# Output projection and norm moved into the attention heads' block, routed masks made by halves

## The chip, the cores and the metric

One core of a Trainium2 chip. The metric is the device time of one execution in microseconds; three runs of the kernel before gave a median of 1414.84 us (1413.32 to 1418.07).

## The reference

Two layers on 1024 tokens of width 256, each made of two attention-like parts and one feed-forward part, all with a residual and a layer norm without weights in front:

```python
x = x + attn_a0(layernorm(x))     # 16 heads of 16, biases and gates
x = x + ternary_ffn(layernorm(x)) # weights rounded to -1, 0, 1 times a scale
x = x + gated_delta(layernorm(x)) # linear attention, 6 heads
x = x + ternary_ffn(layernorm(x))
x = x + attn_a1(layernorm(x))     # 16 heads of 16, no mask
x = x + routed_ffn(layernorm(x))
x = x + latent_attn(layernorm(x)) # causal, rotary, 16 heads
x = x + routed_ffn(layernorm(x))
```

An attention part ends in `out = ctx @ Wproj.T + bproj`. The routed part is one shared gated feed-forward (704 hidden features) with a low-rank addition for each of 8 experts, of which each token takes two:

```python
topw, sel = jax.lax.top_k(x @ gate_w.T, 2)
topw = softmax(topw, axis=1)            # over the tokens
lo_up = 2 * (xt @ up_A[e].T @ up_B[e].T)
h_e = silu(base_up + lo_up) * (base_gate + lo_gate)
mixed_h += c[:, None] * h_e             # c: weight of expert e for this token
out = mixed_h @ w_down.T + lora_down
```

## The kernel before

Tokens lie in 8 tiles of 128 rows in `X` (`x_tokens`), their normed values, turned, in `XNT` (`xn_features`, two tiles of 128 features by 1024 tokens). Each part of the network is a block in which five engines run streams written by hand; semaphores order them, and no engine begins the next block before all have ended this one. PSUM has 8 banks of 512 columns.

**Heads** (`attention_heads`, from line 483; used by `attention16` and by `latent_attention`). 128 chunks (16 heads by 8 key tiles): PE makes scores, ACT takes their exp, PE multiplies by the values. Banks 4 to 6 are a ring that the row maxima's scores and the small `turn` steps share; bank 7 holds a head's sum. At the end ACT copies the last head's sum, `turn(HEADS + 1)` transposes it and DVE divides it (L695, L698) into `O` (`attended`).

**Projection** (`project_out`, L1113). A block of its own: PE transposes `O` in 4 groups of 4 (L1138), ACT copies each (L1155), PE multiplies each tile by `wo` (two products of 256 columns, L1145), DVE adds it to `X` (L1163). The next routed weights are loaded by SP in this block (in the second `attention16` only).

**Norm** (L77). By pairs of tiles: DVE takes statistics (L95) and aggregates (L100); ACT the root (L147); DVE the reciprocal (L105), the shift (L107) and the odd tile's rows (L109); ACT the even tile's rows (L150); PE transposes both (L161, 4 transposes) into bank p; ACT copies 512 columns to `XNT` (L142, `take`). In the projection PE does the first pair's transposes behind tile 5 (`pe_behind`), and ahead of the last pair one unread product of 512 columns (`keep_busy`, L173). ACT takes the roots in the order of the pairs, each behind the copy of the pair before last. Norms stand at the end of the loading of inputs, both ternary parts, the gated part's `project_out` (three products for each tile), both `attention16`, the first routed part and the latent part.

**Routed part** (`routed_ffn`, L2176). PE begins with the four first-rank products of token half 0 (`lora_part`, L2243, two records of 512 columns each) between the 8 tiles' logits (L2270), then the base products of pair 0 (L2258), the sum over rows (L2275), base products of pair 1. DVE meanwhile takes logits, top two, indices, the softmax's parts, and spreads each token's expert and weight over 128 columns, 16 instructions of 128 columns each (L2414, L2423). PE transposes these 32 tiles (L2286), ACT copies them (L2375), DVE subtracts the masks (L2435, 1024 columns) and masks the first-rank products (L2431). Then steps (p, k) for 11 pairs of feature tile and token half and for two slots: PE adds the second-rank products (L2309), ACT takes silu (L2383), DVE the gate product (L2443) and the hidden values (L2448), POOL the mix (L2363). The order of steps is (0,0), (1,0), (0,1), (2,0), (1,1) and so on; pairs share 3 sets of two banks.

## Time and profile before

| | us |
|---|---|
| median of 3 runs | 1414.84 |
| profiled execution | 1413.13 |
| its span | 1411.1 |
| PE busy | 1325.0 |
| DVE busy | 893.1 |
| ACT busy | 689.3 |

The span is the time from the first to the last instruction of the profiled execution. Busy shares are averages over stages; the granted clock of PE is 0.985 of 2.4 GHz over the whole span, with the 11th, 12th and 15th of 40 slices at 0.8.

### The profile page before, as it was taken

Reading aid. Unit: us, or ns where it says so; the run is one execution under the profiler, and the core shown is the slowest. Engines: PE = TensorE matmul, PEld = TensorE weight load, DVE = VectorE, ACT = ScalarE, POOL = GpSimd, SP = SyncE. Lnnn points to the kernel's source line nnn. Section 1 sums busy time; section 2 is a strip of 40 time slices with the busy share of each in tenths; the row PEclk is TensorE's granted clock in tenths of the full one; section 3 lists DMA queues with packets and bytes.
Section 4 is the critical chain, followed back from the end, with each engine's and each line's share of the span. In section 5 each row is a group of like instructions: output and inputs, shape, how many; then the busy total and the mean of one; then the engine's idle time right before and its main releaser. Section 6 shows DMA issues by size and latency. Waiting matters only on the chain. (4 is left out here: it accounts for less than half of the span.)

```text
span 1411.1 us, 33212 instructions
## 1 busy us (share of the span) xinstructions
PE 1325.0 (94%) x13887; PEld 741.7 (53%) x13895; DVE 893.1 (63%) x2159; ACT 689.3 (49%) x1038; POOL 278.5 (20%) x343
## 2 busy tenths in 40 slices
PE   8999998999679988999999989999899999989999
PEld 4455554475346774644555554446355555654436
DVE  5999993757486456759999736433656556526431
ACT  5678786636483226546777842111444444442110
POOL 5340522001420000052000000111533434200110
PEclk9999999999889989999999999999999999999999
DMA  4323300000300000032222030001200000000000
GB/s 98 67 42 69 66 3 21 15 2 1 120 1 4 16 1 16 1 64 36 36 36 36 2 118 0 1 0 26 46 13 19 14 14 15 8 1 0 0 0 30
DMA packets 33526, 37.50 MB, mean 27 GB/s; under 512 B 8722, under 2 KB 24194, under 8 KB 33378
## 3 DMA queue, kind: packets, MB, share of 16 engines
q1 hardware_dynamic: 33376, 35.38, 12.2%
q8 instruction: 110, 1.80, 0.5%
q14 instruction: 38, 0.31, 0.1%
q10 hardware_dynamic: 2, 0.00, 0.0%
HBM read 18.43 MB, written 1.07 MB: 14 GB/s over the span
## 5 line engine op out<-in xcount | busy, mean ns | idle before, releaser
L677 DVE TENSOR_REDUCE row_max_pieces<-psum 128x1 f32<-128x512 f32 (+3 forms) x672 | 406.9, 646 | 103.2 <-PE psum L565 101.2
L778 ACT ACTIVATE probs<-psum 128x1024 f32<-128x1024 f32 (+7 forms) x384 | 343.4, 900 | 199.9 <-PE psum L565 199.4
L624 PE MATMUL psum<-probs,v_ones 128*32 128x256 f32 (+1 forms) x2880 | 236.4, 362 | 8.8 <-POOL probs L554 4.4
L565 PE MATMUL psum<-q_all,k_head 97*32 97x512 f32 (+3 forms) x1536 | 176.9, 487 | 0.0
L565 PE MATMUL psum<-k_stack,q_stack 96*32 96x512 bf16 x2048 | 159.8, 379 | 3.3 <-issue 3.2
L565 PE MATMUL psum<-q_stack,k_stack 97*32 97x512 bf16 x2048 | 158.0, 379 | 2.0 <-issue 1.8
L624 PEld LDWEIGHTS psum<-probs,v_ones 128*32 128x32 f32 x2880 | 95.5, 109 | 87.7 <-POOL probs L554 24.3
L565 PEld LDWEIGHTS psum<-k_stack,q_stack 96*32 96x32 bf16 x2048 | 57.7, 95 | 65.6 <-DVE row_max_pieces L677 12.2
L565 PE MATMUL psum<-k_head_bf,q_all_bf 80*32 80x512 bf16 (+3 forms) x768 | 84.0, 328 | 3.3 <-ACT k_head_bf L2625 1.0
L565 PEld LDWEIGHTS psum<-q_stack,k_stack 97*32 97x32 bf16 x2048 | 58.5, 96 | 51.7 <-ACT probs L778 4.3
L565 PEld LDWEIGHTS psum<-q_all,k_head 97*32 97x32 f32 x1536 | 75.8, 109 | 18.0 <-issue 2.6
L2383 ACT ACTIVATE silu<-psum 128x512 f32<-128x512 f32 x44 | 26.3, 597 | 118.6 <-PE psum L2309 118.6
L2309 PE MATMUL psum<-lora_in,arena 128*128 128x512 f32 (+1 forms) x192 | 80.0, 595 | 3.4 <-DVE lora_in L2431 3.4
L2443 DVE TENSOR_TENSOR gate_weighted<-psum,weight_rows 128x512 f32<-128x512 f32 (+1 forms) x48 | 33.1, 691 | 78.6 <-PE psum L2309 78.5
L2258 PE MATMUL psum<-xn_features,arena 128*128 128x512 f32 (+1 forms) x192 | 79.5, 595 | 0.0
L565 PEld LDWEIGHTS psum<-k_head_bf,q_all_bf 80*32 80x32 bf16 x768 | 36.2, 95 | 44.5 <-DVE row_max_pieces L677 8.7
L554 POOL TENSOR_SCALAR_AFFINE_SELECT probs<-probs 128x128 f32<-128x128 f32 x128 | 36.9, 292 | 106.0 <-ACT probs L778 106.0
L2363 POOL TENSOR_TENSOR mixed_hidden<-slot_hidden 128x512 f32<-128x512 f32 x22 | 27.9, 1267 | 149.4 <-DVE slot_hidden L2448 149.4
L2309 PEld LDWEIGHTS psum<-lora_in,arena 128*128 128x128 f32 (+1 forms) x192 | 32.2, 181 | 46.8 <-issue 39.8
L2258 PEld LDWEIGHTS psum<-xn_features,arena 128*128 128x128 f32 (+1 forms) x192 | 32.2, 181 | 41.3 <-issue 39.8
L2734 POOL TENSOR_TENSOR q_all<-by_cos_over_by_sin,by_sin_moved 64x512 f32<-64x512 f32 x32 | 41.2, 1286 | 51.5 <-ACT by_sin_moved L2728 48.2
L379 PE MATMUL psum<-xn_parts,w_up_signs 128*128 128x512 bf16 x186 | 47.0, 379 | 2.9 <-DVE hidden L454 2.6
(380 smaller groups left out, 2060.8 us busy)
## 6 DMA issues: line engine op xcount, KB each, us to landing
q_stack<-arena SPq DMA_DIRECT2D x32, 96.0 KB, 2.7
k_stack<-arena SPq DMA_DIRECT2D x32, 96.0 KB, 3.0
arena<-gd_g_sums SPq DMA_DIRECT2D x6, 512.0 KB, 6.0
k_stack<-arena SPq DMA_DIRECT2D x32, 64.0 KB, 2.6
q_stack<-arena SPq DMA_DIRECT2D x32, 64.0 KB, 2.7
x_tokens<-in_x SPq DMA_DIRECT2D x4, 256.0 KB, 3.8
k_stack<-arena SPq DMA_DIRECT2D x32, 32.0 KB, 2.2
q_stack<-arena SPq DMA_DIRECT2D x32, 32.0 KB, 2.7
```

The source lines that it names most:

```text
L379: last = pe.matmul(psum[:, 2 * b + j, :], w[:, k, e * P:(e + 1) * P], XP[:, part, k, cols(half)], start=(part == 0 and k == 0), stop=(part ...
L554: pool.affine_select(out=own, in_=own, compare_op=ALU.is_ge, fill=0.0, base=0, pattern=[[1, P]], channel_multiplier=-1).then_inc(masked, 1)
L565: last = pe.matmul(o[j:j + 32], by[:, j:j + 32], rows, **flags)
L624: last = pe.matmul(psum[32 * g:32 * g + VW, PVB, first * P:end * P].rearrange("p (b n) -> p b n", n=P), V[:, c, h, :], by_group(pr[:, n % ...
L677: last = dve.reduce_max(mx[:, h % 2, qt, i:i + 1], o[:, 0:plain], AX.X)
L778: act.activation(pr[:, n % PB, q_from(c):], psum[:, 2 * (n % 2):2 * (n % 2) + 2, :].rearrange("p a n -> p (a n)")[:, q_from(c):], ACT.Exp, ...
L2258: pe.matmul(psum[rows, 2 * (p % BUF) + j, :], w[wb][:, kk, features], XNT[:, kk, cols], start=(kk == 0), stop=False, skip_group_check=True)
L2309: last = pe.matmul(psum[rows, 2 * (p % BUF) + j, :], w[wl][:, features], Z[:, j, k, cols], start=False, stop=True, skip_group_check=True)
L2363: pool.tensor_tensor(MX[:, f, cols], H[:, 0, f, cols], H[:, 1, f, cols], ALU.add).then_inc(mixed, 1)
L2383: act.activation(sil[:, i % 2, :], psum[:, 2 * (p % BUF), :], ACT.Silu).then_inc(silu, 1)
L2443: last = dve.tensor_tensor(gc[rows, i % 2, :], psum[rows, 2 * (p % BUF) + 1, :], CB[rows, k, cols], ALU.mult)
L2734: pool.tensor_tensor(Q[0:RD, h % QSLOTS, cols(half)], t[0:RD, (i + 2) % 3, :], moved[:, (i + 2) % 3, :], ALU.add).then_inc(added, 1)
```

## The change

- `project_out` is no longer used by the three attention parts with heads. A new class `HeadsOut` does its work in the streams of `attention_heads`: first half of the features of token half 0 transposed behind the last values, of half 1 behind the last `turn`; the rest after DVE has divided the last head. Products go to banks 0 to 3, the norm's transposes to banks 4 to 7. ACT copies three of the four groups of features, DVE one.
- There the norm is behind all 8 products (`behind=NT - 1`), and `lagging`: the last pair's root comes ahead of the third pair's rows, and 8 products of 128 columns that nobody reads (`fill`) stand ahead of the second and the third pair's transposes. The gated part's `project_out` has the same with `fill=6`.
- All norms but the first are `split`: the last pair's two feature tiles go to two banks, one copied by ACT, one by DVE.
- The logits of tiles 0 to 3 are computed at the end of the block before (`afterwards`), those of tiles 4 to 7 at the routed block's start, ahead of the first-rank products.
- Masks and weights are spread, transposed and copied by token halves; half 0 before step (0,0), half 1 between (0,0) and (1,0) on PE. The masking of the second half moves from behind step 0 to behind step 1 on DVE. Step (0,0) waits for two masked products, not four.
- POOL clears old semaphores in the heads' blocks (ahead of the first mask in the causal one), SP loads the routed weights behind the heads' own loads. In the latent part SP no longer waits for `wo`; PE does.

```diff
@@ Norm.dve_behind, act, pe, pe_behind
         if t == NT - 1:
             dve.wait_ge(added, NT)
             self.stats(dve, NT - 1)
+            self.moments(dve, self.PAIRS - 1)
             self.inverse(dve, self.PAIRS - 2)
-            self.moments(dve, self.PAIRS - 1)
             self.inverse(dve, self.PAIRS - 1)
+            self.take_last(dve)
...
+    def take_last(self, dve):
+        if self.split:
+            p = self.PAIRS - 1
+            dve.wait_ge(self.turned, p + 1)
+            out, turned = self.half_of_pair(p, 1)
+            dve.tensor_copy(out, turned).then_inc(self.taken_last, 1)
...
+        for p in range(self.PAIRS):
+            if not (self.lagging and p == self.PAIRS - 1):
+                root(p)
+            if self.lagging and p == self.PAIRS - 2:
+                root(p + 1)
             act.wait_ge(self.shift_done, p + 1)
...
             for p in range(behind // 2 + 1, self.PAIRS):
-                if p == self.PAIRS - 1 and self.early:
+                if self.lagging:
+                    if 0 < p < self.PAIRS - 1:
+                        self.warm(pe, self.fill, self.bank + p)
+                elif p == self.PAIRS - 1 and self.early:
...
                 self.pe(pe, p)
+            if self.afterwards:
+                pe.wait_ge(self.taken, 2)
+                self.afterwards(pe, 0)
@@ attention_heads, tensor stream
+                pe.wait_ge(ring_out, turn_place(HEADS - 1) + 1)
+                out.turn(pe, out_bank(0), 0, 0)
                 turn(HEADS + 1)
+                pe.wait_ge(ring_out, turn_place(HEADS) + 1)
+                out.turn(pe, out_bank(1), 0, 1)
+                pe.wait_ge(ring_out, turn_place(HEADS + 1) + 1)
+                out.pe(pe, out_bank)
@@ class HeadsOut
+    def pe(self, pe, bank):
...
+        pe.wait_ge(self.first_kept, 1)
+        self.turn(pe, bank(0), 1, 0)
+        self.product(pe, 0, 0)
+        pe.wait_ge(self.first_kept_late, 1)
+        self.turn(pe, bank(1), 1, 1)
+        pe.wait_ge(self.second_kept, 1)
+        self.product(pe, 0, 1)
+        for t in range(1, NT):
+            if t >= 4:
+                pe.wait_ge(self.second_kept, 2)
+                pe.wait_ge(self.added, t - 3)
+            for k in range(KT):
+                self.product(pe, t, k)
+        self.norm.pe_behind(pe, NT - 1)
...
@@ routed_ffn, tensor stream
+                    for t in range(4, NT):
+                        last = logits_of(pe, core, w, t)
+                    last.then_inc(lg_in, 1)
...
+                    for j in range(2):
                         for k in range(KT):
+                            lora_part(0, j, k)
                     pe.wait_ge(tot, 1)
-                    pe.matmul(psum[:, 5, P:P + TOPK], core.ones_sq[:], ps_[:], ...
+                    pe.matmul(psum[:, 3, 0:TOPK], core.ones_sq[:], ps_[:], ...
+                    base_part(0, 0)
+                    turn_rows(0, 0)
+                    pe.wait_ge(lg_out, 1)
+                    base_part(0, 1)
+                    turn_rows(1, 0)
                     for p, k in steps:
                         half, f = pairs[p]
                         if (p, k) == (1, 0):
+                            pe.wait_ge(tot_read, 1)
+                            base(1)
+                            turn_rows(0, 1)
+                            turn_rows(1, 1)
                             lora_in(1)
...
-                        if k == 0 and f == 0:
-                            pe.wait_ge(z_done, 2 * TOPK * (half + 1))
+                        if f == 0:
+                            pe.wait_ge(z_done, 2 * TOPK * half + 2 * (k + 1))
@@ routed_ffn, vector stream
                     def lora_masked(half):
...
+                        dve.wait_ge(kept, 2 * TOPK * half + TOPK)
+                        dve.tensor_tensor(MD[:, cols], MASK[:, 1, cols], MASK[:, 0, cols], ALU.subtract)...
+                        for k, m in enumerate((MASK[:, 0, cols], MD[:, cols])):
+                            for j in range(2):
...
                     lora_masked(0)
+                    for kind in range(2):
+                        spread(kind, 1)
+                    dve.wait_ge(kept, 2 * TOPK)
...
-                        if i == 0:
+                        if i == 1:
                             lora_masked(1)
+                            dve.wait_ge(kept, 2 * TOPK * NH2)
```

## Rows read from the trace of the kernel before

**Rows 1.** The page's part 1: busy us (share of the span) and instructions of each engine.

```profile
PE 1325.0 (94%) x13887; PEld 741.7 (53%) x13895; DVE 893.1 (63%) x2159; ACT 689.3 (49%) x1038; POOL 278.5 (20%) x343
```

**Rows 2.** Timeline at the second transition: start us, us, engine, line, names, count, idle before.

```profile
818.35 0.35 DVE L698 TENSOR_TENSOR attended<-psum,reciprocals 128x64 f32<-128x64 f32 x2
...
823.54 0.42 DVE L1163 TENSOR_TENSOR x_tokens<-psum,x_tokens 128x256 f32<-128x256 f32 x1 [4.83 <-PE psum L1145]
...
826.99 0.42 DVE L1163 TENSOR_TENSOR x_tokens<-psum,x_tokens 128x256 f32<-128x256 f32 x1
...
827.67 0.15 DVE L105 RECIPROCAL rstd<-std 128x2 f32<-128x2 f32 x1
...
828.25 0.41 DVE L1163 TENSOR_TENSOR x_tokens<-psum,x_tokens 128x256 f32<-128x256 f32 x1
...
830.26 0.42 DVE L1163 TENSOR_TENSOR x_tokens<-psum,x_tokens 128x256 f32<-128x256 f32 x1 [1.13 <-PE psum L1145]
...
834.31 0.17 DVE L105 RECIPROCAL rstd<-std 128x2 f32<-128x2 f32 x1 [0.86 <-ACT std L147]
...
836.05 0.60 ACT L142 ACTIVATE xn_features<-psum 128x512 f32<-128x512 f32 x1 [0.26 <-PE psum L161]
```

**Rows 3.** Chain of waits that ended last, in the last layer: start us, us, what.

```profile
1285.88 2.49 DVE lora_in L2431 x4
```

**Rows 4.** Timeline of the first routed layer's start, up to step (1,0).

```profile
843.30 0.95 PE L2270 MATMUL psum<-arena,xn_features 128*128 128x8 f32 x8
...
844.29 0.23 DVE L2397 COPY logits<-psum 128x64 f32<-128x64 f32 x1 [9.29 <-PE psum L2270]
...
847.15 3.22 DVE L2414 TENSOR_SCALAR wide_rows<-arena,indices_f 128x128 f32<-128x128 f32 x16
...
851.28 1.04 PE L2286 MATMUL psum<-identity,wide_rows 128*128 128x128 f32 x8
...
858.18 1.98 PE L2309 MATMUL psum<-lora_in,arena 128*128 128x512 f32 x4 [1.72 <-DVE lora_in L2431]
...
863.43 3.60 PE L2309 MATMUL psum<-lora_in,arena 128*128 128x512 f32 x8
```

**Rows 5.** Stretches of 2 us: their length, then PE, PEld, DVE, ACT, POOL busy, PEclk, DMA.

```profile
816.00:818.00 2.00, 1.13 (x14) 0.36 (x10) 0.00 (x0) 0.76 (x2) 0.00 (x0) 1.00 0.00 0
...
820.00:822.00 2.00, 2.00 (x11) 2.00 (x10) 0.00 (x0) 1.49 (x3) 0.00 (x0) 0.50 0.45 107
...
1250.00:1252.00 2.00, 2.00 (x12) 2.00 (x11) 0.00 (x0) 1.20 (x2) 0.00 (x0) 0.50 0.00 0
```

**Rows 6.** Timeline of the first transition.

```profile
226.18 0.35 DVE L698 TENSOR_TENSOR attended<-psum,reciprocals 128x64 f32<-128x64 f32 x2
...
226.87 1.94 PE L1138 MATMUL psum<-identity,attended 128*128 128x128 f32 x16 [0.96 <-PEq L542]
...
230.02 0.42 DVE L1163 TENSOR_TENSOR x_tokens<-psum,x_tokens 128x256 f32<-128x256 f32 x1 [3.48 <-PE psum L1145]
...
242.53 0.60 ACT L142 ACTIVATE xn_features<-psum 128x512 f32<-128x512 f32 x1 [0.26 <-PE psum L161]
```

**Rows 7.** Timeline at the third transition and the last layer's step (1,0).

```profile
1248.74 0.35 DVE L698 TENSOR_TENSOR attended<-psum,reciprocals 128x64 f32<-128x64 f32 x2
...
1293.67 3.60 PE L2309 MATMUL psum<-lora_in,arena 128*128 128x512 f32 x8
```

**Rows 8.** Timeline at the end of the gated layer's projection.

```profile
539.36 0.60 ACT L142 ACTIVATE xn_features<-psum 128x512 f32<-128x512 f32 x1 [0.26 <-PE psum L161]
```

**Rows 9.** Timeline of POOL, SP and PE around old semaphores' clearing and the first mask.

```profile
836.92 0.38 SPq L2489 DMA_DIRECT2D w_latents<-in_m_w  x1
...
845.54 0.38 POOL L2358 PARTITION_ALL_REDUCE all_max<-part_max  x1 [200.06 <-DVE part_max L2402]
...
1020.45 1.03 POOL L2696 CAST k_features_bf<-k_features 128x1024 bf16<-128x1024 f32 x1
...
1024.62 0.64 PE L624 MATMUL psum<-probs,v_ones 128*32 128x256 f32 x8
```

More of the change, by code:

```diff
@@ L141, in take, with root @@
             act.wait_ge(self.turned, p + 1)
+            if self.split and p == self.PAIRS - 1:
+                out, turned = self.half_of_pair(p, 0)
+                act.activation(out, turned, ACT.Copy).then_inc(self.taken, 1)
+                return
             act.activation(core.XNT[:, :, 2 * p * P:(2 * p + 2) * P],
-                           core.psum[:, p, :].rearrange("p (f n) -> p f n", f=KT), ACT.Copy).then_inc(self.taken, 1)
-        for p in range(self.PAIRS):
+                           core.psum[:, self.bank + p, :].rearrange("p (f n) -> p f n", f=KT), ACT.Copy).then_inc(self.taken, 1)
+        def root(p):
             act.wait_ge(self.mv_done, 2 * p + 2)
@@ L196, in load_inputs @@
     with ExitStack() as tmp:
-        norm = Norm(core, "in", tmp)
+        norm = Norm(core, "in", tmp, split=False)
         spare = core.sb("spare_root", [P, 1], F32, tmp)
@@ L1118, in project_out @@
         OT = core.sb("attended_features", [P, tiles, S], F32, tmp) if OT is None else OT
-        norm = Norm(core, tag, tmp, xn, 1, behind=4)
+        norm = Norm(core, tag, tmp, xn, 1, behind=4, lagging=True, fill=6)
         with nc.Block() as block:
@@ L2173, in routed_weights, with logits_of, routed_early, early @@
     return w, loads, router_loaded, loaded, 16 * (4 + 3 + 2 * 3)
+LOGITS_BANK = 1
+def logits_of(pe, core, w, t):
+    for k in range(KT):
+        last = pe.matmul(core.psum[:, LOGITS_BANK, t * NX:(t + 1) * NX], core.XNT[:, k, t * P:(t + 1) * P],
+                         w["gate"][:, k, :], start=(k == 0), stop=(k == KT - 1))
+    return last
+def routed_early(core, w, router_loaded):
+    def early(pe, half):
+        if router_loaded:
+            pe.wait_ge(router_loaded, 32)
+        for t in range(4 * half, 4 * half + 4):
+            logits_of(pe, core, w, t)
+    return early
 def routed_ffn(nc, core, tag, w, router_loaded, loaded, all_loaded, next_loads, out_dram=None):
@@ L2276, in _ @@
[L2276 to L2289 removed]
+                    pe.matmul(psum[:, 3, 0:TOPK], core.ones_sq[:], ps_[:], start=True, stop=True).then_inc(tot_in, 1)
```

196 lines of the change are left out of this document (129 added, 67 removed).

## The prediction

> **What bounds the kernel now.** I read the page's busy shares first [rows 1]: PE is busy 94% of the span and every other engine has slack, so time can only come from PE's gaps, from work taken off PE, or from its clock. Next the timeline at the three places where an attention stage hands over. There the order of work is a chain and not a full PE: after DVE has normalised the last head (0.35 us from 818.35, so at 818.70, which I call zero of the second transition) the first projected tile is added at 823.54, DVE then waits 1.13 us for a product [rows 2], waits 0.86 us for a root (834.31), and the last copy of ACT starts at 836.05 and takes 0.60. Then the chain of waits in the routed layer [rows 3]: mask products of DVE stand on the path, and the first product of masked rows starts at 858.18, 13.9 us after the logits reach DVE at 844.29 [rows 4]. Last the granted clock [rows 5]: 0.50, so 1.2 GHz, in 820 to 822, after a stretch in which PE was busy 1.13 of 2 us, and 0.50 again in 1250 to 1252, in the third transition.
>
> The zeros of the first and third transitions are 226.18 + 0.35 = 226.53 [rows 6] and 1248.74 + 0.35 = 1249.09 [rows 7].
>
> **Projection and norm in the heads' block (three places).** Removed: one block boundary, and the order in which PE put the first pair's transposes ahead of the last two tiles' products. I work on the second transition's zero, at 2.4 GHz. A transpose takes 0.107 us at this clock (16 in 1.94 with the tail of the last [rows 6]), a product of 256 columns 0.427 (two records of 0.213, the same rate), so a tile 0.853.
> - Start. Of the 16 transposes of the attended features 8 need only heads 0 to 7: four fill PE's wait for ACT's last copy, four run while DVE normalises head 15. After zero PE does 4 transposes (0.43), ACT copies them (0.60) behind a lag of about 0.25, and meanwhile PE does the first half product and 4 more transposes. The second half product starts near 1.5, the first add at 2.2. Before: 4.84 here, 3.49 in the first transition [rows 2, 6], which has the same instructions at full clock; the 1.35 between them is the price of the low clock.
> - Adds follow at 3.10, 3.96, 4.81, 5.67 by PE's 0.853. From there DVE is behind its own work: an add with the statistics behind it takes 0.68, a pair's inverse 0.58 (826.99, 827.67 and 828.25 in [rows 2]), two aggregates 0.16. Tiles 5, 6 and 7 start at 6.92, 7.77 and 9.03; the last statistics end at 10.26, moments of the last pair 10.5, inverse of pair 2 and of pair 3 begin at 10.46 and 11.04. Before, the last inverse began at 15.6 (834.31).
> - The root moved up: the last pair's root is computed at 10.6 while DVE does pair 2's inverse, so the 0.86 wait goes. It delays pair 2's row copy on ACT by nothing measurable (0.28 us root, done as the shift arrives).
> - PE: products end at 7.9, transposes of pair 0 8.3, eight small products of 128 columns (two records each, 0.213) 10.0, pair 1 10.5, eight more 12.2, pair 2 12.6, pair 3 13.05. The second eight are on the path: pair 2's rows are ready at 11.5, so they cost 0.5 us at the last copies. The old unread product (two records, 0.86) goes.
> - The last copy: 256 columns each on ACT and DVE, 0.42 for what takes 0.60 [rows 2]. It starts near 13.3 and ends at 13.75. Before, the last copy ended at 17.95 here and at 16.60 in the first transition [rows 6].
> First transition: the next block's PE waits for these copies in both kernels: 16.60 - 13.75 = 2.85, of which I take **2.8**. It is not less than about 2 (if both groups of small products land on the path) and not more than 3.5 (if neither does).
>
> **Logits early, routed masks by halves (two places).** The logits of four tiles (16 records of 0.107, 1.7 us [rows 4]) run behind pair 3's transposes, to 14.8, under the last copies. The new block's PE starts at 15.2 and does the other four, so DVE has the logits at 17.2; before at 25.6 (844.29), because four first-rank products (eight records of 0.427, 3.43; the eight of the row of 863.43 in [rows 4] take 3.60 with their tail) stood between them. From there the small chain is unchanged: 2.86 us to the spreading of rows (847.15, sixteen in 3.22 us, so 0.2 each), of which now only eight (1.6) come before the first transposes. PE in order: logits to 16.9, four first-rank products to 20.4, sum 20.5, half of base products 22.3, eight transposes (1.04 with their tail [rows 4], 0.86 by pitch) 23.1, other half 24.9, eight transposes 25.7. DVE: both halves' first rows copied by ACT at 24.0, difference of 512 columns 0.69, two masked products 0.6 apart: the first step may begin at 26.2. PE waits 0.5 here. Then the step (1.72) 27.9, base of pair 1 (3.43) 31.35, sixteen transposes with one wait of 0.5 to 0.6 for ACT's copies between them 33.6, first-rank products of the second half 37.0, and step (1,0) begins. Before, it began at 863.43 - 818.70 = 44.7, and in the last layer at 1293.67 - 1249.09 = 44.6 [rows 4, 7]; behind it both kernels run the same products back to back. So **7.7** and **7.6**.
> The cross-check goes by PE's work: from zero to step (1,0) PE has 35.3 us of work after the change (16 small products included) and 1.7 us of gaps in my sum, 37.0; nothing can take it under 35.3, which bounds the gain at 9.4 each. From the other side, a low clock as in [rows 5] takes 1.35 off, and a full exposure of both waits for ACT and DVE (another 1.5) leaves 4.8.
> Moved past queues: the routed weights' loads now stand behind the heads' own loads on SP's queue, so they start some 10 us earlier, and land before anyone waits for them in both kernels: nothing. The adding of the second half's masks moves behind step 1 on DVE; what is queued behind it is step (0,1), which PE needs for its buffer only one pair (6.9 us) later: nothing; it would cost up to 2.4 if that cover were gone.
>
> **Small ends.** The gated layer's projection gets the earlier root, the split copy and six small products (1.28 us) between pairs 1 and 2, where PE waits about as long anyway: root and product waits gone, the last copy, which before begins at 539.36 [rows 8], ends 0.6 earlier: **0.6** (0 to 1). Three other norms only get the split copy: 0.18 each, **0.5** (0 to 0.6).
>
> **POOL.** In the causal heads' block POOL now clears the old semaphores before its first mask. The trace has no row of a clearing. Its bounds: nothing, and 8.6 us, since in the routed layer it was over when POOL started the all-reduce at 845.54, in a block that began at 836.92 (SP's first load, [rows 9]). POOL is free at 1021.5 and the first product that needs the mask starts at 1024.62 [rows 9], so up to 2.6 us are free and the loss is 0 to 6.0. I take 0: none of it has a busy record, so its length is unknown, and most of the cheap end is covered by the free 2.6 us.
>
> **Sum.** 2.8 + 7.7 + 7.6 + 0.6 + 0.5 = 19.2 us off. The profiled run took 1413.1 us (span 1411.1): 1393.9. The median shown is 1414.8, 1.7 above this run, so a median after of **1395** is my value.
>
> **The clock.** At two transitions the trace shows 1.2 GHz for some 3 us after a half-idle stretch [rows 5]; at the first, with the same instructions, 2.4 GHz throughout (first add at 3.49). PE's gaps between the last values and the first product shrink from about 2 us to about 0.8. So I take full clock at all three.
> The Trainium skill (TensorE: Matmul & The Clock Gate, Part 1: The HAM clock gate) says that the engine is throttled by default and that only activity releases it; by this rule filling the gaps with work keeps 2.4 GHz, and a phase that happens to catch the remaining gaps would still throttle it. The rows show both outcomes for one instruction sequence, which agrees with it.
>
> **Rivals.**
> - Low clock again at one or both routed transitions. For it: the rows of two of three transitions. Against: half of the gaps filled. It gives back 1.35 each, and some of the small products at 0.43 instead of 0.21: 1396.5 to 1399. Chance 0.2.
> - POOL's clearing delays the causal heads' first masks: up to 6.0, so 1396 to 1401. For it: 30 or more semaphores, on one engine, ahead of a product in PE's order. Chance 0.1.
> - The gain stays in the norms: the masks' order adds waits that I don't see (each half waits for two copies of ACT, which alternates with its own silu work). Then each routed transition gives only what its norm gives, 17.95 - 13.75 = 4.2, and the sum is 12.3: 1402.5; with both low clocks (2.7) and POOL's 6.0 on top 1411.2, which is half of its chance and within 0.3% of before. Against it: every wait found has its cover above. Chance 0.06.
> - Slower than before: PE falls to 1.2 GHz in the new sequence of short products and transposes and does not come back until the long products. PE's 35.3 us between zero and step (1,0) would double; it decides from 19 us lost in all, that is when each of the two routed transitions runs more than 9.6 us of PE's work at half clock. That gives 1415 to 1450. Against it: the clock came back within 3 us of steady work. Chance 0.03.
> - My forecast: chance 0.61, own range 1392 to 1397.
>
> What a measurement of this kernel can tell from no change is about 0.3%, 4.2 us. Range: 1391 to 1401, the clock and POOL cases within. Faster 0.94, within 0.3% 0.03, slower 0.03.
>
> **What would show it.** First add about 2.2 us after the last head's normalising, not 3.5 or 4.8; no root wait before the last reciprocal; the last copies as two of 256 columns side by side; logits at DVE some 8.4 us earlier after zero; step (1,0) at 37 after zero; the granted clock near 1.00 in the slices of the second and third transitions; the causal layer's first mask within 2.6 us of POOL's last cast. A first step that starts later than 28 after zero, or a transition with 0.50 in its clock column, would make the prediction wrong by the prices above.

## The result, and the profile after

The changed kernel takes 1403.2 us in the median (1401.42 to 1405.84, 6 runs), the kernel before in the same comparison 1414.1 (1410.06 to 1418.07, 6 runs): ratio 0.9926, 95% interval 0.9901 to 0.9950. The forecast was 1395 with a range of 1391 to 1401. The sign was right; of the 19.2 us forecast 10.9 came. The profiled execution took 1405.0 us, its span 1403.3.

The page's first part for the kernel after (busy time and share of the span) shows PE as full as in [rows 1]:

```profile
PE 1334.0 (95%) x13987; PEld 754.0 (54%) x13995; DVE 897.1 (64%) x2171; ACT 685.8 (49%) x1035; POOL 278.0 (20%) x343
```

**The norm came as forecast.** Timeline of the kernel after, second transition (start, duration, engine, line, instruction, idle time before it). Zero is 816.38 + 0.35 = 816.73; the rows answer to [rows 2]:

```profile
816.38 0.35 DVE L743 TENSOR_TENSOR attended<-psum,reciprocals 128x64 f32<-128x64 f32 x2
...
818.94 0.42 DVE L904 TENSOR_TENSOR x_tokens<-psum,x_tokens 128x256 f32<-128x256 f32 x1 [1.61 <-PE psum L856]
...
827.14 0.30 ACT L168 ACTIVATE std<-mean_var,norm_eps 128x2 f32<-128x2 f32 x1 [0.46 <-DVE mean_var L103]
...
827.37 1.95 PE L198 MATMUL psum<-identity 128*128 128x128 f32 x16
...
827.59 0.16 DVE L108 RECIPROCAL rstd<-std 128x2 f32<-128x2 f32 x1
...
829.16 1.04 PE L191 MATMUL psum<-identity,qk_rest 128*128 128x128 f32 x8
...
830.23 0.42 DVE L152 COPY xn_features<-psum 128x256 f32<-128x256 f32 x1 [1.97 <-PE psum L191]
830.29 0.38 ACT L161 ACTIVATE xn_features<-psum 128x256 f32<-128x256 f32 x1
```

First add 2.21 after zero (forecast 2.2, before 4.84), last inverse at 10.86 with no wait for the root in front of it (11.04), last copies two at once, done at 13.94 (13.75, before 17.95). All 14 profiles of kernels with the new projection show this first add, at 2.13 to 2.31, at all three transitions, at 2.4 GHz.

**The routed start did not.** The same view of the two routed starts of the kernel after. Zero is 816.73 for the first part and 1244.07 for the second; they answer to [rows 4, 7, 9]:

```profile
835.45 0.22 DVE L2565 COPY logits<-psum 128x64 f32<-128x64 f32 x1 [4.79 <-PE psum L2319]
...
836.39 0.18 DVE L2570 TENSOR_REDUCE part_max<-sorted 128x2 f32<-128x16 f32 x1
...
838.67 0.37 POOL L2523 PARTITION_ALL_REDUCE all_max<-part_max  x1 [195.17 <-issue]
...
839.14 0.17 DVE L2575 TENSOR_TENSOR exp_top<-sorted,all_max 128x16 f32<-128x16 f32 x1 [1.48 <-POOL all_max L2523]
...
846.57 1.98 PE L2474 MATMUL psum<-lora_in,arena 128*128 128x512 f32 x4 [0.19 <-DVE lora_in L2606]
...
1262.41 0.18 DVE L2570 TENSOR_REDUCE part_max<-sorted 128x2 f32<-128x16 f32 x1
...
1266.59 0.37 POOL L2523 PARTITION_ALL_REDUCE all_max<-part_max  x1 [24.60 <-issue]
...
1267.07 0.18 DVE L2575 TENSOR_TENSOR exp_top<-sorted,all_max 128x16 f32<-128x16 f32 x1 [3.38 <-POOL all_max L2523]
...
1267.82 0.38 PE L2445 MATMUL psum<-part_sum,ones_square 128*128 128x2 f32 x2 [2.85 <-DVE part_sum L2579]
...
1275.01 1.90 PE L2474 MATMUL psum<-lora_in,arena 128*128 128x512 f32 x4
```

The first masked product, step (0,0), starts 29.8 and 30.9 after zero; the forecast was 26.2, before it was 39.5. Two things stand in the rows. From the start of `part_max` to the start of the all-reduce of the top value it is 2.3 and 4.2 us; before it was 0.3. "<-issue" says that GpSimd waited for nothing that the profile names: its own queue held it. The other is the clock. Stretches of the kernel after around the first routed start (after the length: busy us of PE, PEld, DVE, ACT and POOL, the granted clock, DMA's share and GB/s; the last row is from the third transition):

```profile
830.00:832.00 2.00, 1.88 (x18) 1.79 (x16) 0.42 (x1) 0.67 (x2) 0.00 (x0) 1.00 0.00 0
832.00:834.00 2.00, 1.82 (x11) 1.85 (x11) 0.00 (x0) 1.28 (x1) 0.00 (x0) 0.63 0.36 99
834.00:836.00 2.00, 2.00 (x8) 1.74 (x9) 0.52 (x6) 0.00 (x0) 0.00 (x0) 0.50 0.31 77
...
1268.00:1270.00 2.00, 2.00 (x6) 0.93 (x7) 1.93 (x11) 0.00 (x0) 0.00 (x0) 0.86 0.00 0
```

In the second transition 1.2 GHz begins at 832.5 (15.8 after zero), before anybody waits for GpSimd, and lasts to 839.4. In the third it begins only at 1269.4, behind the wait, and lasts 3.4 us. So there are two candidates, and the trace alone can't price either. What it can show is what GpSimd did. The rows of the all-reduce's line in the window of each routed start, first around 832, then around 1260 (duration in ns, then first and last start):

```profile
L2523 POOLq MODIFY_POOL_CONFIG  x2: 11/11/11, 832.9 to 833.0; - x2
...
L2523 POOLq MODIFY_POOL_CONFIG  x2: 11/14/16, 1260.7 to 1260.7; - x2
```

GpSimd's queue passes an instruction there that stands in no line of the kernel's text and lasts 11 ns, and the all-reduce comes 5.7 and 5.9 us later. The ternary layer has the same thing in the other direction: its all-reduce is over at 84.85, and the next ordinary operation, which needs nothing else, starts at 91.64:

```profile
84.40 0.45 POOL L352 PARTITION_ALL_REDUCE abs_totals<-abs_sums  x1 [31.28 <-ACT magnitudes L338]
91.64 0.18 POOL L353 TENSOR_TENSOR abs_totals<-abs_totals 128x2 f32<-128x2 f32 x1 [6.80 <-issue]
```

I call this the switch of GpSimd's code. The row alone is no proof of a wait: at 32.55, between two ordinary operations, the same 11 ns row stands and the next operation follows 0.2 us behind it. The wait comes where the all-reduce follows or precedes. The Trainium skill (GPSIMD Engine Reference, 2.1 Instruction dispatch) describes it: the first call to a freshly loaded kernel costs about 6 us more, with no visible instruction. The rows here agree, with 5.6 to 7.0 over the profiles in which the all-reduce had to wait for it. The kernel before has the switch's row too, here at its second transition:

```profile
L2358 POOLq MODIFY_POOL_CONFIG  x2: 11/11/11, 837.7 to 837.7; - x2
```

Its all-reduce had its value only at 845.5 [rows 9], so the switch had 7.8 us of cover, and 7.3 in the third transition. After the change `part_max` ends 3.6 and 1.9 us behind the switch (836.57 and 1262.59), which needs 5.7 and 5.9.

The clearing of old semaphores, which the prediction held to have no row, has one. These are its rows in the kernel before at the first routed start, and then in the kernel after at the second:

```profile
L73 POOLq EVENT_SEMAPHORE_RANGE_CLEAR  x2: 45/134/223, 837.0 to 837.3; - x2
...
L73 POOLq EVENT_SEMAPHORE_RANGE_CLEAR  x4: 45/80/242, 1259.6 to 1260.3; - x4
```

It is over 0.5 us after the block's first load at 836.92 and, in the kernel after, 0.3 us ahead of the switch's row.

### The profile page after: what moved, and what is told of

It is laid out like the page before. It is cut to its first block and busy times, and to the rows that moved or that the text cites. A ratio compares the mean times of both kernels' runs of the same rounds, so it can differ in the third digit from the quotient of the medians.

```text
span 1403.3 us, 33400 instructions
## 1 busy us (share of the span) xinstructions
PE 1334.0 (95%) x13987; PEld 754.0 (54%) x13995; DVE 897.1 (64%) x2171; ACT 685.8 (49%) x1035; POOL 278.0 (20%) x343
## 3 DMA queue, kind: packets, MB, share of 16 engines
q1 hardware_dynamic: 33376, 35.38, 12.3%
## 5 line engine op out<-in xcount | busy, mean ns | idle before, releaser
L1349 PE MATMUL psum<-xn_features,identity 128*128 128x512 f32 x80 | 46.0, 689 | 4.7 <-DVE t_blocks L1429 3.1
```

What stands on the lines that cost most here:

```text
L1349: pe.matmul(psum[:, bank_of, :], ident[:], XNT[:, 0, 0:HALF], start=True, stop=True)
```

## The experiments

All times are medians; the kernel before was measured beside each group of runs, at 1412.1 to 1413.0. Kernels of different groups are best compared by their ratios, whose intervals are mostly some 0.25% to either side; what is smaller than that is read from the traces. The code is shortened.

**1. Clearing or switch.** GpSimd's first work in the routed block is the clearing of old semaphores, which the prediction had named as the unknown. It was moved behind the all-reduce:

```diff
-                    core.clear_retired()
                     pool.wait_ge(pmax, 1)
                     pool.partition_all_reduce(gm[:], pm[:], P, ...).then_inc(gmax, 1)
+                    core.clear_retired()
```

> The changed kernel, with GpSimd's clearing of old semaphores moved behind the all-reduce of the top value in the two routed blocks. In the changed kernel's trace the all-reduce starts 6.5 and 7.1 us after its block does, 2.1 and 4.0 us after the value it needs (part_max), and DVE idles 1.48 and 3.38 us for it. Theory A (the switch of GpSimd's code: the rows MODIFY_POOL_CONFIG at 832.9 and 1260.7 start 5.8 and 5.9 us before the all-reduce, the clearing ends before them): the all-reduce comes only 0.8 to 1.2 us earlier, PE's idle of 2.85 us in the third transition shrinks by about 1, time 1401.5 to 1403.5. Rival B (the clearing itself takes the 6.5 to 7 us): the all-reduce starts right behind part_max, DVE's waits go, PE's idle goes, time 1397 to 1399.

1401.9 us (1400.46 to 1405.22). The all-reduce stays late: 7.3 and 6.1 us after the block's start, and DVE still idles for it.

```profile
836.03 0.18 DVE L2570 TENSOR_REDUCE part_max<-sorted 128x2 f32<-128x16 f32 x1
840.36 0.37 POOL L2522 PARTITION_ALL_REDUCE all_max<-part_max  x1 [195.91 <-issue]
840.83 0.18 DVE L2575 TENSOR_TENSOR exp_top<-sorted,all_max 128x16 f32<-128x16 f32 x1 [3.52 <-POOL all_max L2522]
```

The switch instruction came at 833.4, 0.3 after the block's start where it had come 0.8 after it with the clearing in front: the clearing costs half a microsecond. Rival B is out; the rows of the clearing above say the same. The same shows where the prediction had looked for it, in the causal heads: the kernel after clears there from 1016.6 to 1017.5, and the first mask at 1017.61 follows the exp that ends at 1017.26 by 0.35 us, where it followed by 0.1 before.

**2. The switch made early.** The switch's rows bear the line of the instruction behind them, so it stands ahead of the first instruction of the other kind. With an unread all-reduce at the end of GpSimd's work in the heads' blocks it moves there:

```diff
+    def pool_end(self, pool):               # end of GpSimd's stream in the heads' block
+        pool.memset(spare[0][:], 0.0)...
+        pool.partition_all_reduce(spare[1][:], spare[0][:], P, ...)
```

> The changed kernel, plus an all-reduce of a spare pair of columns that nobody reads, at the end of GpSimd's work in the heads' blocks ahead of both routed layers; with it the program holds no switch of GpSimd's code at the start of the routed blocks, since the code is already the all-reduce's. The clearing stays where it is. Theory A (switch): the all-reduce starts within 0.3 us of part_max at both places, DVE's idle of 1.48 and 3.38 us goes, PE's idle of 2.85 us in the third transition goes and the 1.2 GHz stretch behind it (1269 to 1273) with it, some 1.5 us more; in the second transition PE is slow at 832.5 to 839 and works without a gap, so nothing is won there. Time 1397.5 to 1399.5. Rival B (clearing): the all-reduce stays at 6.5 to 7 us behind the block's start, time 1403. Rival C (the clock falls for PE's earlier gaps, whatever the wait is): DVE's waits go, the 1.2 GHz stretches stay, time 1400 to 1401.

1401.5 us (1400.4 to 1405.45), ratio 0.9919 (0.9894 to 0.9943). The unread all-reduce's line has the switch now, 5.8 us ahead of it at both places, and the routed all-reduce has none:

```profile
L922 POOLq MODIFY_POOL_CONFIG  x4: 11/11/16, 643.0 to 1239.6; - x4
L922 POOL PARTITION_ALL_REDUCE spare_pair_top<-spare_pair x2: 371/371/371, 648.8 to 1245.3; - x2
```

The routed all-reduce starts 0.28 us after `part_max` does at both places, and DVE waits no more. Timeline, second transition (zero 815.45) and third (zero 1241.36):

```profile
834.07 0.35 POOL L2534 PARTITION_ALL_REDUCE all_max<-part_max  x1 [184.88 <-DVE part_max L2581]
...
841.95 1.55 PE L2485 MATMUL psum<-lora_in,arena 128*128 128x512 f32 x3 [0.20 <-DVE lora_in L2617]
...
1260.87 0.35 POOL L2534 PARTITION_ALL_REDUCE all_max<-part_max  x1 [15.18 <-DVE part_max L2581]
...
1271.22 1.12 PE L2485 MATMUL psum<-lora_in,arena 128*128 128x512 f32 x2 [0.19 <-DVE lora_in L2617]
```

One transition is the forecast come true: 2.4 GHz throughout, step (0,0) at 26.5 (forecast 26.2), step (1,0) at 37.5 (37.0). In the other PE ran at 1.2 GHz from 1257.6 to 1264.5 and step (0,0) came at 29.9. The same instructions, so 3.4 us is the low clock's price here by itself. The waits went as theory A has it, the low clock stayed in one place of two as rival C has it. The median's gain on the changed kernel, 1.7 us, is within the intervals; the trace carries the reading:

```profile
1256.00:1258.00 2.00, 1.70 (x15) 1.64 (x14) 0.00 (x0) 1.23 (x1) 0.00 (x0) 0.91 0.00 0
1258.00:1260.00 2.00, 2.00 (x9) 1.94 (x10) 0.32 (x3) 0.06 (x1) 0.00 (x0) 0.50 0.04 8
1260.00:1262.00 2.00, 2.00 (x3) 0.67 (x2) 1.93 (x27) 0.00 (x0) 0.35 (x1) 0.50 0.00 0
```

**3. No all-reduce at all.** The other way to take the wait away; `part_max` and the all-reduce itself are left out too:

```diff
-                    dve.wait_ge(gmax, 1)
-                    dve.tensor_tensor(ev[:], m8[:, :, 0:TOPK], gm[:]..., ALU.subtract).then_inc(dif, 1)
+                    dve.tensor_copy(ev[:], m8[:, :, 0:TOPK]).then_inc(dif, 1)
```

> The changed kernel without the top value: the two all-reduces, part_max and the subtraction of the top value are left out (the exponentials are taken of the logits as they are, which gives the same weights but for rounding, as long as the logits are small). This takes away everything that DVE could wait for on GpSimd in the small chain, whichever of switch and clearing it is. Theories A and B: as the kernel with the early switch or 0.3 us faster per place, 1396.5 to 1399.5. Rival C (clock alone): 1400 to 1401.

1403.2 us (1400.53 to 1406.62), no better than the change. DVE waits for nobody, but the clock fell at both starts (0.52 and 0.50), and step (0,0) came at 28.2 in both. Its profiled run has the latest first zero of all, 230.5. No theory had its time in range. I had tied the low clock to the wait, and it comes without it.

**4. The routed layer of before behind the new projection.** `routed_ffn` of the kernel before, and `next_early=None` at both places.

> The changed kernel with the routed layer of the kernel before (first-rank products between the logits, masks not by halves, no logits of the next layer behind the norm): only the projection and norm in the heads' block, the small unread products, the split copies and the earlier root are left. The prediction's terms for these sum to 2.8 + 4.2 + 4.2 + 0.6 + 0.5 = 12.3 us, so 1401.8 from the median 1414.1. If these terms hold, the routed layer's part of the change is worth nothing in the changed kernel as it is (1403.2), its 6.9 us having been eaten by the wait for GpSimd and the low clock. If the routed part is worth what the prediction gave it and the norm's terms are the ones that failed, this kernel takes 1407 to 1410.

1405.6 us (1404.44 to 1408.99), ratio 0.9947 (0.9925 to 0.9968). That lies between the two numbers. Beside the kernel before of its own group the gain is 7.0 us, where 12.3 were forecast for these terms. The trace shows where they are: logits at DVE at 21.6 and 21.4 after zero, and step (1,0) at 42.4 and 40.6, where the norm's terms alone give 44.7 - 4.2 = 40.5; at the first of the two PE had 1.2 GHz in 852 to 856. So the norm's terms hold. What the profile lacks against them is 3.0 us in the first 229 us, which experiment 5 takes up, and 1.9 for that low clock. The routed layer's own part, forecast at 3.4 to 3.5 a place (7.7 and 7.6 less 4.2), gave 1.6 and -1.2 in the changed kernel's profile (step (1,0) at 40.8 and 41.8), and the 1.6 only against a start with that low clock in it.

**5. Two identical kernels.** The kernel before once more, as one of the kernels compared.

> The kernel before, unchanged, as a second profile of it and as a measure of what two identical kernels differ by. In the five kernels with the change the first transition's zero lies at 227.17 to 230.50 us, in the one profile of the kernel before at 226.53, though the instructions ahead of it are the same; the granted clock is low at 28 to 36 us in four of the five and in none of before. Theory (a phase of the clock that a run happens on, not the change): this second profile may show a zero anywhere in 226.5 to 230.5; the time is within 0.3% of before. Rival (the change itself slows the first 230 us): zero at 226.5 again, within 0.3 us.

1413.3 us against 1412.1: ratio 1.0012 (1.0002 to 1.0023). Two identical kernels differ by more than their interval, so an interval that misses 1 by less than some 0.1% says nothing. The changed kernel's profile had its first zero 3.0 us later than the kernel before (229.57 against 226.53), though nothing ahead of it was touched. Over 16 profiles of all kernels the rows explain it. The program starts with 32 unread products; here they are in the kernel after, and then in the profile of experiment 9 that repeats it:

```profile
3.84 6.72 PE L198 MATMUL psum<-identity 128*128 128x128 f32 x32
```

```profile
3.84 5.69 PE L198 MATMUL psum<-identity 128*128 128x128 f32 x32
```

They last 5.17 to 6.78 us. Where they last 6.02 or less (7 profiles) the zero is that time plus 221.2, within 0.05. Where they last 6.19 or more (9 profiles) PE has 1.2 GHz within 29 to 36 us as well, and the zero lies at 229.0 to 230.5. So which of the two courses an execution takes, some 3 us apart, can be told from its first ten microseconds. The changed kernel took both (229.57 here, 226.91 in experiment 9), so the change doesn't fix the course. Both profiles of the kernel before took the short one; whether the change makes the long one more frequent is not shown.

**6. What holds the clock.** Three kernels, all with the early switch. First the logits of two tiles in the place of the second group of small products:

```diff
-                        self.warm(pe, self.fill, self.bank + p)      # between pairs 1 and 2
+                        pe.wait_ge(self.taken, 1); self.afterwards(pe, (0, 1))
...
-                self.afterwards(pe, 0)                               # tiles 0 to 3
+                self.afterwards(pe, (2, 3))
```

> The kernel with the early switch of GpSimd's code, and in the projection ahead of a routed layer the second group of small unread products is replaced by the logits of tiles 0 and 1, which need only pair 0; the logits of tiles 2 and 3 stay behind pair 3's transposes. Beside the last copies PE then has 0.95 us of logits instead of 1.85, and pair 2's transposes, which in the trace start 1.05 us after their rows are there, behind the small products, start about 1.0 earlier. Main theory (path lengths): the next block starts 14.0 to 14.3 after zero instead of 15.4, the logits are at DVE at 16.0 to 16.3 instead of 17.4, 1.2 us gained at both places, time 1399 to 1400.5. Rival (the clock: fewer columns through PE ahead of the routed block): 1.2 GHz in both transitions for some 6 us, which costs 2 to 3.4 us a place, time 1402 to 1405.

1402.1 us (1399.34 to 1405.51). Path lengths came (last copies done at 13.4, block at 14.0), and the clock fell in both: step (0,0) at 28.5 and 26.8, where the earlier block gives 25.1 by path (25.94 less 0.86, from experiment 8). The rival's mechanism, at 3.4 and 1.7 us.

Next a first-rank product among the logits:

```diff
+                        if t == 6: lora_part(0, 0, 0)
                         last = logits_of(pe, core, w, t)
```

> The kernel with the early switch, and in the routed block one first-rank product (two records of 512 columns, 0.86 us) stands between the logits of tiles 5 and 6 instead of behind those of tile 7. The same products in another order. In eight routed starts of kernels with the change that were profiled, the clock was at 1.2 GHz somewhere in 14 to 22 us after zero in seven (all but the second transition of the kernel with the early switch). Theory (the run of 32 logits of 8 columns each, with the block's start in it, brings the clock down): with a long product among them 1.00 throughout in both transitions, step (1,0) at 37.6 to 38.3 after zero, time 1398 to 1401. Rival (it isn't the short columns but the gap at the block's start, or plain chance): the clock falls as before in at least one of the two, step (1,0) at 40 to 41 there, time 1401 to 1403.

1404.8 us (1401.19 to 1407.06), the wrong way: 1.2 GHz for 10 and 7 us, step (0,0) at 31.7 and 29.9. My theory of that moment fell.

Then no small products at all after the heads (`fill=0`):

> The kernel with the early switch and without the small unread products between the pairs of the norm that follows the heads (16 of 128 columns at each of three places left out). Theory by path lengths: the last copies end about 0.7 us earlier at each place (pair 2's transposes start 1.05 us after their rows now, pair 3's rows then set the end), 2 us in all, time 1399 to 1400. Rival (the products hold the clock): 1.2 GHz from about 8 us after zero on at all three places, 2 to 4 us each, time 1404 to 1410.

1409.3 us (1407.01 to 1416.07), ratio 0.9983 (0.9973 to 0.9994): the small products that look like waste are worth 7.8 us against experiment 2. In its first transition:

```profile
240.00:242.00 2.00, 1.09 (x6) 0.86 (x7) 0.79 (x4) 1.99 (x4) 0.00 (x0) 0.86 0.00 0
242.00:244.00 2.00, 1.21 (x5) 0.78 (x4) 0.85 (x2) 0.94 (x2) 0.00 (x0) 0.50 0.00 0
```

PE was busy for about half of these stretches, and 1.2 GHz came at all three transitions, from 12 to 14 after zero on, for 7 to 14 us. This profiled run was the slowest of its eleven, so the traces show more loss than the median has.

**7. Where the logits stand.** All eight tiles' logits in the routed block, in a row, or woven with first-rank products as before (and the first base products ahead of the total):

```diff
-                    for t in range(4, NT):
+                    for t in range(NT):
+                        if t % 2 == 0: lora_part(0, t // 4, t // 2 % KT)      # woven only
                         last = logits_of(pe, core, w, t)
```

> The kernel with the early switch, but no logits behind the norm: all eight tiles' logits stand in a row at the start of the routed block, then the four first-rank products as in the changed kernel. In eleven of twelve profiled routed starts of kernels with early logits the clock fell to 1.2 GHz between 14 and 20 us after zero; in the kernel with the old routed layer (no early logits, first-rank products woven between the logits) it did not in either transition. By path lengths the block starts at 14.2 after zero, DVE has the logits at 17.7, step (0,0) starts at 26.8 and step (1,0) at 37.8. Theory P (it is the row of logits of 8 columns, wherever the block's boundary lies): the clock falls again in both transitions, step (0,0) at 29 to 31, time 1400 to 1403. Rival Q (it is the logits' place in the norm, beside the last copies): 1.00 in both, step (0,0) at 26.8, time 1396 to 1399.

> The kernel with the early switch, no logits behind the norm, and in the routed block the order of the kernel before (a first-rank product of 512 columns ahead of every second tile's logits), with the first base products of the first pair ahead of the total so that PE has work in that wait; the masks by halves stay. By path lengths: logits at DVE 21.5 after zero, total 24.4, step (0,0) at 29.8, step (1,0) at 40.7. Theory P (the row of short logits brings the clock down): 1.00 throughout, step (0,0) at 29.8, time 1400 to 1402, as good as the changed kernel though its chain is 3 us longer. Rival (chance of phase): the clock falls in at least one of the two and step (0,0) comes at 31 to 33 there, time 1402 to 1405.

In a row: 1402.4 us (1399.91 to 1405.55); the clock fell in both transitions from 19 after zero, step (0,0) at 28.8 against 26.8 by path. Theory P: the place in the norm is not the cause. Woven: 1406.2 us (1403.18 to 1407.65); 1.00 through the whole start, step (0,0) at 30.0 in one, in the other 1.2 GHz for 3 us from 27 after zero, step (0,0) at 31.2. It holds the clock over the logits, as in the kernel with the old routed layer, but costs more path than the low clock does.

**8. One long unread product.** The order of experiment 6 with a product of 512 columns between the last transposes and the last two tiles' logits, under the last copies:

```diff
+                self.keep_busy(pe, 2, 1)
                 pe.wait_ge(self.taken, 2)
-                self.afterwards(pe, 0)
+                self.afterwards(pe, (2, 3))
```

> The kernel with the early switch and the logits of tiles 0 and 1 in the place of the second group of small products, and one unread product of 512 columns (0.86 us) between pair 3's transposes and the logits of tiles 2 and 3, where PE would otherwise be one product ahead of the last copies. By path lengths: block at 14.9 after zero, logits at DVE 16.9, step (0,0) at 26.0 and step (1,0) at 37.0. Theory R (more columns beside the last copies hold the clock): 1.00 in both, time 1397 to 1400. Rival P (the rows of short logits on both sides of the boundary bring it down all the same): 1.2 GHz from 14 to 20 in at least one, step (0,0) at 27.5 to 30 there, time 1400 to 1403.

1399.7 us (1394.91 to 1402.17), ratio 0.9910 (0.9890 to 0.9931). The granted clock is 1.00 through both transitions, step (0,0) at 25.94 and 25.95, step (1,0) at 36.9 in both.

**9. Chance or order, and the switch by itself.** The changed kernel again, the kernel of experiment 8 without the early switch, and the kernel of experiment 8 again, on one chip:

> The changed kernel, unchanged, timed beside the two below. Theory: 1403.2 within 1.5 us; DVE waits for GpSimd's all-reduce at both routed starts again (all-reduce 6.5 to 7.2 us behind the block's start), the clock falls in at least one of the two starts, and the first transition's zero lies at 226.5 to 230.5 by the length of the 32 unread products at the start (5.4 to 6.8 us). Rival: the waits were peculiar to one run, zero of either here.

> The changed kernel with the logits of tiles 0 and 1 between pairs 1 and 2 and one unread product of 512 columns behind pair 3, but without the early switch of GpSimd's code. The kernel with both kept 2.4 GHz and had step (0,0) at 25.9 after zero in both transitions. Theory (the switch costs by itself): block at 14.85, all-reduce 5.8 to 6.3 us after the instruction that switches, so at 21.3 to 22 instead of 18.1 after zero, step (0,0) at 28.5 to 30, PE idle for 2.5 to 3.5 us, and behind that idle perhaps 1.2 GHz; time 3 to 4 per place over the kernel with both, less what run-to-run hides: 1404 to 1407. Rival (the switch matters only together with the low clock, and the order alone makes the gain): step (0,0) at 26 to 27, time within 1.5 us of the kernel with both.

> The kernel with the early switch, two tiles' logits between the pairs and one unread product of 512 columns, a second time, beside the changed kernel. Theory: 2.4 GHz in both transitions again, step (0,0) at 25.9 and (1,0) at 36.9 after zero, 3 to 4 us faster than the changed kernel in the medians of this call. Rival (the clock held by chance in one profile, as it did once in the second transition of the kernel with the switch alone): 1.2 GHz in at least one transition here, time within 2 us of the changed kernel.

The changed kernel: 1402.8 us (1400.28 to 1404.64), ratio 0.9929 (0.9903 to 0.9954); the all-reduce starts 2.9 and 3.7 us behind `part_max`, the clock falls in both starts, step (0,0) at 29.8 and 29.9. Its first zero is at 226.91, against 229.57 in its first profile. Without the early switch: 1404.0 us (1399.39 to 1407.99), ratio 0.9932 (0.9906 to 0.9958). Its second transition (zero 816.74) is the clean case for the switch's price, since the clock stays at 1.00:

```profile
834.52 0.18 DVE L2574 TENSOR_REDUCE part_max<-sorted 128x2 f32<-128x16 f32 x1
838.11 0.37 POOL L2527 PARTITION_ALL_REDUCE all_max<-part_max  x1 [194.61 <-issue]
...
839.33 0.38 PE L2449 MATMUL psum<-part_sum,ones_square 128*128 128x2 f32 x2 [2.25 <-DVE part_sum L2583]
...
845.20 1.13 PE L2478 MATMUL psum<-lora_in,arena 128*128 128x512 f32 x2 [0.20 <-DVE lora_in L2610]
```

```profile
834.00:836.00 2.00, 2.00 (x6) 0.86 (x5) 1.76 (x25) 0.00 (x0) 0.00 (x0) 1.00 0.14 41
836.00:838.00 2.00, 1.08 (x3) 0.19 (x1) 0.00 (x0) 0.00 (x0) 0.00 (x0) 1.00 0.00 0
```

Step (0,0) at 28.46 against 25.94 with the early switch: 2.5 us for one switch at 2.4 GHz. At the other place (28.76, with 1.2 GHz for 3 us in it) it is 2.8. With both: 1395.8 us (1393.56 to 1401.75), ratio 0.9885 (0.9857 to 0.9913). Timeline (zero 814.10) and stretches of its second transition:

```profile
826.87 1.02 PE L204 MATMUL psum<-qk_rest,identity 128*128 128x512 f32 x2
...
832.17 0.35 POOL L2538 PARTITION_ALL_REDUCE all_max<-part_max  x1 [184.15 <-DVE part_max L2585]
...
840.04 1.98 PE L2489 MATMUL psum<-lora_in,arena 128*128 128x512 f32 x4 [0.19 <-DVE lora_in L2621]
```

```profile
828.00:830.00 2.00, 1.70 (x17) 1.64 (x16) 0.00 (x0) 1.05 (x1) 0.00 (x0) 1.00 0.04 11
830.00:832.00 2.00, 2.00 (x12) 1.42 (x12) 0.98 (x11) 0.23 (x1) 0.00 (x0) 1.00 0.46 130
```

The starts were the same to 0.01 us as in experiment 8. So the early switch and the long product give four starts out of four at 2.4 GHz; without the long product the clock fell in 13 of 14 (the seven profiles with early logits and small products), in twelve of them 15 to 19 after zero, in the third transition of the kernel after at 25, behind PE's idle. Over both experiments this kernel has a median of 1397.8 (12 runs), the changed kernel 1403.2 (12 runs): it beats both kernels.

## Why the prediction was wrong

- **Projection and norm** (2.8, and 4.2 of each routed place): right. Measured 2.6 (the next block's PE work at 14.3 after zero instead of 16.9) and 4.0 at each of the others. The second group of small products costs 0.55 at the last copies (13.94 against 13.39 without it), forecast 0.5. No clock loss at the first adds, as assumed, where three of four routed transitions in the two profiles of the kernel before had one. The fourth shows what that is worth: without it step (1,0) came at 43.0 after zero, not 44.6. So some 1.5 us of each of the forecast 7.7 and 7.6 was a low clock of the kernel before, and hung on its coming.
- **Small ends** (0.6 and 0.5): not contradicted. With the first transition's 2.8 they make 3.9; from the first zero to the second the profile pair shows 592.17 - 587.16 = 5.0, and the two profiles of before differ there by 0.6.
- **POOL's clearing, 0 of 0 to 6.0**: right in size, but "the trace has no row of a clearing" was wrong, and so the bound of 8.6 us came from the wrong thing. The clearing's rows end at 837.4, and the switch's row follows at 837.7: the rest of the 8.6 was the switch and the wait for `part_max`. Both could have been read before the change was made.
- **The step that failed: "From there the small chain is unchanged: 2.86 us to the spreading of rows".** It was not: 4.3 us in the second transition and 6.2 in the third (`wide_rows` first at 839.75 and 1267.68, logits at 835.45 and 1261.47). The chain had a hidden partner on GpSimd whose end was fixed to the block's start, not to the logits. It had 7.8 and 7.3 us of cover, and the change left 3.6 and 1.9. By itself it costs 2.5 us a place (experiment 9, one place at 2.4 GHz).
- **The second failed step: "So I take full clock at all three".** I looked at the place where the clock had been low before (0 to 4 after zero), where it was cured, and not at the new row of short products behind it. The first rival had a low clock, but at 1.35 a place and a chance of 0.2; the rival "slower than before" had the right place, the new sequence of short products, but gave it 0.03, since it counted only with more than 9.6 us of work at half clock. It came in 13 of 14 starts, at 1.7 to 3.4 us a place where the path at 2.4 GHz is known (experiments 2, 6 and 7); the mixed order of experiment 6 lost up to 5.2 against experiment 2, its own longer path included.
- **The two don't add.** While PE runs at 1.2 GHz it has work left, and the wait for GpSimd lies beside it: in the second transition step (0,0) came at 29.8 where 26.5 was to be had, 3.3 for both together. In the third PE finished its work and idled 2.85 us, then had 1.2 GHz for 3.4 us behind that, 4.4 in all. So the two places gave 3.9 and 2.8 (step (1,0) at 40.8 and 41.8 against 44.7 and 44.6), not 7.7 and 7.6. With these, the sum is 2.6 + 3.9 + 2.8 + 1.1 = 10.4, against 10.9 measured in the medians; the pair of spans shows 7.8, because the profiled run after lost 3.0 us ahead of its first zero. The medians fit it: either remedy alone brought 1.7 us (the early switch) or nothing (the long product), neither clear of noise, and both together 5.4.
- **Otherwise the sum fits, in part by luck.** In the profile with both remedies the pieces from zero to zero are, against the profile of before: -0.2, -4.4, -7.0 and -7.7, together 19.3 us, where 19.2 were forecast for the change. That it agrees to 0.1 is chance: it is the fastest of that kernel's six runs, the kernel has another order of logits, and two profiles of the kernel before differ by 0.6 to 1.5 in each piece behind the first zero. In the medians this kernel gained 12.5 and 17.2 us in its two groups of runs.
- **A slip in the sum.** 1414.8 less 19.2 is 1395.6, not 1395.

Open: what exactly brings the clock down over the short logits. One long product among them did not hold it, one ahead of them beside the copies did, four times of four with the switch early and once of two with it late. The order is a finding, its reason is not.

## What to carry over

When a chain is shortened, list every engine that has to be ready at its end, and for each what its readiness is counted from: a partner that starts with the block and not with the chain loses its cover first. In this kernel an all-reduce on GpSimd behind ordinary operations needed some 6 us ahead of its first use, and an unread one placed early bought them. Work put in to fill PE's gaps is to be priced with what it holds, not only with its own time.

## What had not been expected of the hardware

- The switch of GpSimd's code shows only as a row of 11 ns in its queue (83 ns on the way back) and as "<-issue" on the next instruction: 5.6 to 7.0 us for the all-reduce, 6.8 to 7.1 at the three places in the ternary part of the kernel after where it switches back.
- It is kept across blocks: with the unread all-reduce in the heads' block the routed block had none, and the all-reduce took 0.35 us, 0.28 after what it waits for.
- Clearing 41 semaphores took about 0.5 us, 59 about 0.9 (the switch's row 0.8 and 1.2 us after the block's start with the clearing in front, 0.3 at both without). In the causal heads' block 40 took 0.9 to 1.0. The time goes with the number of clearing rows, which were two, four and five, more than with that of the semaphores.
- 32 equal products at the program's start took 5.17 to 6.78 us, and their length told whether the next 220 us would take 1.5 to 3.1 us more: the 1.2 GHz at 29 to 36 us lasted 3.4 us in eight of these profiles and 6.8 in the one with 3.1.
